# A two-layer decoder on one core: first projections start on their own weights, constant tables reordered and partly made by GpSimd, ScalarE's function table loaded early

## The reference

```
x = _layernorm(x + _L0_attn_ref(x, ...))        # 16 heads of 8, causal
x = _layernorm(x + _L0_xattn_ref(x, ctx, ...))  # 8 heads of 16, 64 context rows of width 96
x = _layernorm(x + _L0_ffn_ref(x, ...))         # router, 64 experts of width 88, 6 per token, and a shared one
x = _layernorm(x + _L1_attn_ref(x, ...))        # 16 heads of 64, causal
x = _layernorm(x + _L1_xattn_ref(x, ctx, ...))  # 16 heads of 64
x = _layernorm(x + _L1_ffn_ref(x, ...))         # an attention with nested widths, 8 heads of 16
```

```
qkv = x @ Wqkv.T
q, k, v = jnp.split(qkv, 3, axis=-1)          # then heads of 8
dots = einsum('bhid,bhjd->bhij', q, k) * scale
dots = jnp.where(causal_mask, -jnp.inf, dots)
attn = jax.nn.softmax(dots, axis=-1)
out = einsum('bhij,bhjd->bhid', attn, v)
return out @ Wout.T + bout
```

## Time and profile before

| | |
|---|---|
| time, three runs | 1831.59, 1843.01 (median), 1845.01 us |
| profiled execution | 1842.62 us, its span 1840.8 us |
| TensorE busy | 88% of the span |
| VectorE, ScalarE, GpSimd busy | 61%, 45%, 13% |
| granted TensorE clock, mean | 0.957 |
| first matmul, first scores | 20.54 us, 27.09 us |
| p1 until / experts until / p3 until | about 545, 654, 1841 us |

### The profile page before, as it was taken

One profiled execution on the slowest core, in us unless ns is written; L12 is line 12 of the kernel. 1 busy time (PEld: TensorE's weight loads), 2 busy tenths in 40 slices (PEclk: granted clock), 3 DMA queues, 4 the chain that ended last, 5 costly groups with the idle time before them and its releaser, 6 DMA issues.

```text
span 1840.8 us, 41666 instructions
## 1 busy us (share of the span) xinstructions
PE 1619.6 (88%) x17584; PEld 1056.4 (57%) x17616; DVE 1113.8 (61%) x2248; ACT 823.2 (45%) x1515; POOL 233.0 (13%) x392
## 2 busy tenths in 40 slices
PE   3799989999868968999998998998998998998985
PEld 1555555555537735665665665674674665665653
DVE  6187767777663454574575475485386387277353
ACT  1555655656522224444344345345445345435422
POOL 0011101111007600110010011011011011011011
PEclk9999999999978989999999999999999999999997
DMA  8421111111139440010010010011011011000000
GB/s 275 148 103 53 63 49 51 64 56 49 46 116 122 105 143 1 29 54 12 19 64 13 19 56 20 19 41 36 19 41 36 6 54 35 2 24 27 5 1 6
DMA packets 64809, 95.70 MB, mean 52 GB/s; under 512 B 9239, under 2 KB 47105, under 8 KB 63891
## 3 DMA queue, kind: packets, MB, share of 16 engines
q1 hardware_dynamic: 61491, 89.20, 14.6%
q0 software_dynamic: 2560, 3.46, 2.2%
q10 hardware_dynamic: 576, 0.39, 0.1%
HBM read 56.02 MB, written 38.80 MB: 52 GB/s over the span
## 4 chain that ended last, share of the span: by engine, by line
PE 57%; DVE 24%; ACT 7%; issue 6%; POOL 4%; DMA 1%; DVEq 0%; ACTq 0%; SPq 0%; POOLq 0%; PEldq 0%
PE psum L990 7%; PE psum L804 5%; DVE peak L1281 5%; PE psum L898 5%; ACT prob L1158 3%; PE psum L647 3%; PE psum L662 3%; PE psum L672 3%; PE psum L885 3%; PE psum L856 3%; DVE w_shared L1281 3%; PE psum L813 2%; PE psum L799 2%; POOL rstd L1456 2%; DVE kx L1406 2%
## 5 line engine op out<-in xcount | busy, mean ns | idle before, releaser
L1158 ACT ACTIVATE prob<-psum 128x1024 f32<-128x1024 f32 (+1 forms) x352 | 322.6, 945 | 354.2 <-PE psum L793 107.6
L1281 DVE TENSOR_REDUCE w_shared<-psum 128x4 bf16<-128x1024 f32 (+1 forms) x160 | 194.2, 1223 | 189.5 <-PE psum L711 125.0
L1281 DVE TENSOR_REDUCE peak<-psum 128x4 bf16<-128x1024 f32 (+1 forms) x160 | 190.8, 1218 | 18.0 <-PE psum L736 12.7
L1453 POOL TENSOR_TENSOR rstd<-moments,eps 128x2 f32<-128x2 f32 x64 | 15.3, 239 | 1018.6 <-DVE moments L1203 1018.6
L804 PE MATMUL psum<-qt,kt 64*128 64x256 f32 x1024 | 131.4, 376 | 0.0
L898 PE MATMUL psum<-prob,v_big 128*64 128x256 f32 x1024 | 124.6, 385 | 0.2 <-issue 0.2
L804 PEld LDWEIGHTS psum<-qt,kt 64*128 64x128 f32 x1024 | 98.5, 189 | 10.8
L898 PEld LDWEIGHTS psum<-prob,v_big 128*64 128x64 f32 x1024 | 68.0, 136 | 42.9 <-issue 11.9
L1309 DVE TENSOR_TENSOR qt<-qt,psum 128x1024 f32<-128x1024 f32 x32 | 38.3, 1218 | 84.7 <-PE psum L966 84.7
L939 PE MATMUL psum<-prob,va 128*32 128x256 f32 (+1 forms) x1536 | 88.9, 358 | 0.4 <-ACT prob L1158 0.2
L1102 ACT ACTIVATE kt<-psum,b_qk 128x256 f32<-128x256 f32 x128 | 53.6, 470 | 51.4 <-PE psum L662 51.0
(11 more groups left out here) (327 smaller groups left out, 3235.9 us busy)
## 6 DMA issues: line engine op xcount, KB each, us to landing
zd<-kx SPq DMA_DIRECT2D x24, 512.0 KB, 5.6
union<-zd SPq DMA_DIRECT2D x16, 768.0 KB, 4.5
w_late<-ad SPq DMA_DIRECT2D x16, 512.0 KB, 3.6
w_late<-vd SPq DMA_DIRECT2D x16, 512.0 KB, 4.6
ad<-union SPq DMA_DIRECT2D x16, 256.0 KB, 2.2
vd<-union SPq DMA_DIRECT2D x16, 256.0 KB, 2.3
xg<-union SPq DMA_DIRECT2D x16, 192.0 KB, 2.0
w_late<-in_w1T SPq DMA_DIRECT2D x1, 2816.0 KB, 11.1
```

The costliest lines, as they stand in the source:

```text
L1158: nc.scalar.activation(prob_of[a][s][:, slot + 2 * i:slot + 2 * i + 2, 0:n], v.pair(step, i)[:, :, 0:n], ACT.Exp, scale=a.scale).then_inc( ...
L1281: nc.vector.tensor_reduce(dst, src, axis=AX.X, op=ALU.max).then_inc(v.free(step), 1)
```

## The change

SyncE's queue begins with `w0_qkv` and both slots' `x`; the constants, the contexts and the other first weights follow, then `ctx_f`. TensorE waits for `w0_qkv` alone (`first_in`), and for the rest (`weights1_in`) ahead of its second step. ScalarE's queue loads four small strips of `ident` (`own_head`) ahead of the strips of `tri`, and ScalarE then runs one exponential on a column of `w0_qkv`, which brings the table load ahead of the first `qt`. GpSimd clears `wf_o`, `bf_o`, the zeros, `shift` and `rdiag`, and makes `sel_h`, `ident_b`, `upper_b` and `spread_b`; the first `T` step waits for them (`tables_ready`). VectorE makes only what the `S` steps and the masks need, and makes `ident_add`, `ones_x` and `shift` behind the experts' stage.

```diff
@@ tensor_step, kind "T"
+                if v.tag == "p1" and g == 0 and v.first():
+                    pe.wait_ge(tables_ready, 1)
...
@@ vector_step, kind "RN"
+                if v.first():
+                    dve.wait_ge(weights1_in, 16 * len(loads1))
...
-        loads1 = [(w0_qkv[:, :], "L0_Wqkv"), (b0_o[:, :], "L0_bout"), (wx_o, "L0_Wo")]
+        loads1 = [(b0_o[:, :], "L0_bout"), (wx_o, "L0_Wo")]
...
-        moved = [(tri_x[rows32(n), x, :], inp["tri"][rows32(n ^ x)]) for x in range(1, 4) for n in range(4)]
+        moved = [(own_head[r:r + 32, :], inp["ident"][r:r + 32, r:r + 16]) for r in range(0, 128, 32)]
+        moved += [(tri_x[rows32(n), x, :], inp["tri"][rows32(n ^ x)]) for x in range(1, 4) for n in range(4)]
...
@@ block.sync
+            sp.dma_start(w0_qkv[:, :], dram("L0_Wqkv")).then_inc(first_in, 16)
+            for s in AB:
+                load1(sp, s, s)
             for dst, name in consts:
                 sp.dma_start(dst, dram(name)).then_inc(consts_in, 16)
             for s in AB:
-                load1(sp, s, s)
                 load_context(sp, p1, s, s)
+            for dst, name in loads1:
+                sp.dma_start(dst, dram(name)).then_inc(weights1_in, 16)
             load_fold_context(sp, 0)
             sp.wait_ge(cleared, 1)
-            for dst, name in loads1:
-                sp.dma_start(dst, dram(name)).then_inc(weights1_in, 16)
...
@@ run_phase
+                            if tag == "p1" and it == -1 and (step[0], step[1]) != ("Q", L0) and not begun:
+                                eng.wait_ge(weights1_in, 16 * len(loads1))
+                                begun.append(step)
...
@@ block.tensor
-            pe.wait_ge(consts_ready, 1)
-            pe.wait_ge(weights1_in, 16 * len(loads1))
+            pe.wait_ge(first_in, 16)
...
@@ block.scalar
-            act.wait_ge(consts_ready, 1)
+            act.wait_ge(first_in, 16)
+            nc.scalar.activation(warm[:, :], w0_qkv[:, 0:1], ACT.Exp)
+            act.wait_ge(columns_set, 2)
...
@@ block.vector, ahead of p1
-            ms(wf_o[:, :, :], 0.0)
             for s in AB:
-                ms(shift[s][:, :, :], 0.0)
-                ms(rdiag[s][:, :, :], 0.0)
-                ms(xt_nested[s][:, :], 0.0)
...
             dve.wait_ge(consts_in, 16 * (len(consts) + len(moved)))
...
-            last.then_inc(consts_ready, 1)
-            dve.wait_ge(weights1_in, 16 * len(loads1))
+            ts(ident_inf[:, :], ident[:, :], 1.0e28, None, ALU.mult)
+            ts(tri_s[:, 0, :], tri[:, 0:128], -250.0, None, ALU.mult)
+            ts(tri_s[:, 1:3, :], tri_x[:, 1:3, 0:128], -250.0, None, ALU.mult)
+            ts(neg_ident[:, :], ident[:, :], -1.0, None, ALU.mult)
+            ts(tri_t[:, 0, :], tri[:, 128:256], -250.0, None, ALU.mult)
+            ts(tri_t[:, 1:4, :], tri_x[:, 1:4, 128:256], -250.0, None, ALU.mult).then_inc(masks_made, 1)
+            dve.wait_ge(masks_made, 1)
             run_phase(dve, "p1", vector_step)
             experts_vector(dve)
+            ts(ident_add[:, :], ident[:, :], 320.0, None, ALU.mult)
+            for u in AB:
+                cp(ones_x[rows64(u), :, :], ones_g[rows64(u), u, :, :])
+            for s in AB:
+                for r in (0, 64):
+                    for j in range(2):
+                        ts(shift[s][r:r + 32, j, 0:128], ident[r:r + 32, r + 31:r + 32].to_broadcast([32, 128]), -250.0, None,
+                           ALU.mult)
...
@@ block.gpsimd, ahead of p1
+            nc.gpsimd.memset(wf_o[:, :, :], 0.0)
+            nc.gpsimd.memset(bf_o[:, :, :], 0.0).then_inc(cleared, 1)
+            nc.gpsimd.memset(zeros, 0.0).then_inc(cleared, 1)
+            for s in AB:
+                nc.gpsimd.memset(shift[s][:, :, :], 0.0)
+                nc.gpsimd.memset(rdiag[s][:, :, :], 0.0)
+            copy = nc.gpsimd.tensor_copy
+            pool.wait_ge(consts_in, 16 * (len(consts) + len(moved)))
+            copy(sel_h[:, :, :], own_head[:, :].unsqueeze(2).to_broadcast([128, 16, 128]))
+            copy(ident_b[:, :], ident[:, :])
+            copy(upper_b[:, :], upper[:, :])
+            copy(spread_b[:, :, :], stage).then_inc(tables_ready, 1)
             pool.wait_ge(weights1_in, 16 * len(loads1))
```

More of the change, by code:

```diff
@@ L388, in decoder_program @@
         scale_v = sb("scale_v", [128, 4])
+        warm = sb("warm", [128, 1])
+        own_head = sb("own_head", [128, 16])
         by_layer = lambda own, cross: {a: cross if a is L0X else own for a in (L0, L0X, L1, L1X, L1F)}
@@ L433, in decoder_program @@
         weights_in = sem("weights_in")
-        consts_ready = sem("consts_ready")
+        tables_ready = sem("tables_ready")
         zeroed = sem("zeroed")
@@ L1954, in run_phase @@
         def run_phase(eng, tag, do_step, prepare=None):
+            begun = []
             def body(it, aheads):
@@ L2003, in _ @@
             ms, cp, ts = nc.vector.memset, nc.vector.tensor_copy, nc.vector.tensor_scalar
-            ms(wf_o[:, :, :], 0.0)
             for s in AB:
-                ms(shift[s][:, :, :], 0.0)
-                ms(rdiag[s][:, :, :], 0.0)
-                ms(xt_nested[s][:, :], 0.0)
-                ms(peak[s][:, :, :], 0.0)
-                ms(peak_x[s], 0.0)
-                ms(r_sel[s], BIG)
                 ms(va0[s], 0.0)
                 ms(va_x[s], 0.0)
-            ms(bf_o[:, :, :], 0.0).then_inc(cleared, 1)
-            ms(zeros, 0.0).then_inc(cleared, 1)
-            dve.wait_ge(cleared, 1)
+                ms(peak[s][:, :, :], 0.0)
+                last = ms(peak_x[s], 0.0)
+            last.then_inc(columns_set, 1)
+            for s in AB:
+                ms(r_sel[s], BIG)
+            dve.wait_ge(columns_set, 1)
             for s in AB:
@@ L2020, in _ @@
                 for i in range(2):
-                    ms(va_x[s][64 * i:64 * i + 64, :, 32 * i + 16:32 * i + 17], 1.0)
+                    last = ms(va_x[s][64 * i:64 * i + 64, :, 32 * i + 16:32 * i + 17], 1.0)
+            last.then_inc(columns_set, 1)
             dve.wait_ge(consts_in, 16 * (len(consts) + len(moved)))
-            ts(tri_s[:, 0, :], tri[:, 0:128], -250.0, None, ALU.mult)
-            ts(tri_t[:, 0, :], tri[:, 128:256], -250.0, None, ALU.mult)
-            ts(tri_s[:, 1:3, :], tri_x[:, 1:3, 0:128], -250.0, None, ALU.mult)
-            ts(tri_t[:, 1:4, :], tri_x[:, 1:4, 128:256], -250.0, None, ALU.mult)
-            cp(ident_b[:, :], ident[:, :])
-            cp(upper_b[:, :], upper[:, :])
-            cp(spread_b[:, :, :], stage)
-            ts(neg_ident[:, :], ident[:, :], -1.0, None, ALU.mult)
-            ts(ident_inf[:, :], ident[:, :], 1.0e28, None, ALU.mult)
-            ts(ident_add[:, :], ident[:, :], 320.0, None, ALU.mult)
-            for u in AB:
-                cp(ones_x[rows64(u), :, :], ones_g[rows64(u), u, :, :])
             nc.vector.tensor_reduce(slot_mask[:, 0:4], head_mask[:, 0:16].rearrange("p (j i) -> p i j", i=4), axis=AX.X,
@@ L2038, in _ @@
                                     op=ALU.add)
-            for r in range(0, 128, 32):
-                rows = slice(r, r + 32)
-                if r % 64 == 0:
-                    for s in AB:
-                        for j in range(2):
-                            ts(shift[s][rows, j, 0:128], ident[rows, r + 31:r + 32].to_broadcast([32, 128]), -250.0, None,
-                               ALU.mult)
-                last = cp(sel_h[rows, :, :], ident[rows, r:r + 16].unsqueeze(2).to_broadcast([32, 16, 128]))
-            last.then_inc(consts_ready, 1)
-            dve.wait_ge(weights1_in, 16 * len(loads1))
+            ts(ident_inf[:, :], ident[:, :], 1.0e28, None, ALU.mult)
[5 more added lines that the diff above has]
+            dve.wait_ge(masks_made, 1)
             run_phase(dve, "p1", vector_step)
             experts_vector(dve)
+            ts(ident_add[:, :], ident[:, :], 320.0, None, ALU.mult)
[6 more added lines that the diff above has]
+                           ALU.mult)
             for s in AB:
```

3 lines of the change are left out of this document (added).

## The result

The changed kernel takes 1829.64 us (median of 22 runs, 1825.86 to 1837.15), the kernel before on the same chips 1837.07 us (22 runs, 1828.17 to 1845.01). The ratio is 0.9958 with a 95% interval of 0.9946 to 0.997: some 7 us faster, clear of no change and under one per cent. Of the three runs of before that stand in the table two were among its slower ones, and the third (1831.59 us) among its faster; between the medians of 22 the difference is 7.4 us.

What follows compares the result with a forecast made beforehand. Bound: the head's chain, with VectorE's tables ahead of `kt`. Constants 12.4 us, tables to 13.8, GpSimd's hold 3.5, `kt` to scores 2.40: scores 19.7 instead of 27.09 us; 1842.62 - 7.4 = 1835.2 us (chance 0.45), range 1827 to 1843 us.

Steps and rivals of the forecast that it cites:

- the constants: Head: ScalarE's last strip load starts at 7.7 us and takes 4.73 us, so all constants are in at 12.4 us.
- GpSimd's copies: Head: GpSimd's four table copies, 3264 columns, take 4.5 us at half the rate of `x_res` for one input.
- VectorE's loss: Head: beside GpSimd's copies VectorE loses 0.79 us for each us, 3.5 us, so `kt` starts at 17.3 us.
- `kt` to scores: Head: from the start of `kt` to the first scores 2.40 us as before, so the scores come at 19.7 us.
- rival (f): Whole kernel: the change works but runs scatter over it, 13.4 us among three; chance of median over 1% faster 0.06, slower 0.03.
- ScalarE's table load: Head: its 1.28 us are done at 9.4 us, hidden behind the wait for the constants, and cost nothing.
- (a): Head: VectorE isn't held up by GpSimd's copies; 10.8 us gained, 1831.8 us; chance 0.15.
- (b): Head: GpSimd copies at the full rate of `x_res`; 7.0 us lost, 3.9 us gained, 1838.7 us; chance 0.15.
- (e): Head: GpSimd's copies hold VectorE past the old `kt` start, from 4.2 ns per column; 1845.8 us at 5.5 ns; chance 0.05.
- (c): Head: the first weights become the bound, in at 21.6 us; 5.5 us gained, 1837.1 us; chance 0.07.
- (d): Scores: TensorE's clock rise stays at about 57 us, some 2.5 us more at the lower level, 1837.7 us; chance 0.10.
- The experts' end: End of experts' stage: VectorE's 1.8 us of moved tables hide in its 6.33 us wait for routed rows, costing nothing.

Runs made afterwards that it cites:

- the loads alone: Changed kernel, but VectorE makes all tables ahead of `kt` in the order of before and GpSimd none: scores at 25.91 us, ratio 1.0013 to the kernel before.
- the first two experiments: Changed kernel with GpSimd's table copies held until VectorE's masks are made: scores 16.42 us; changed kernel with two more `sel_h`-shaped copies on GpSimd: `kt` at 20.13 us.
- the strips first: Changed kernel with ScalarE's queue loading the `own_head` strips behind those of `tri`, on a semaphore only GpSimd waits for: scores at 17.29 us, single run 1828.44 us.
- GpSimd behind VectorE: Changed kernel with GpSimd's four table copies waiting until VectorE has made its masks: scores at 16.42 us, ratio 0.9947 to the kernel before.
- The three versions with the strips first: Changed kernel with `tri` strips first: scores 17.29 us; plus GpSimd's copies behind masks and a later weights wait: 15.79; plus VectorE waiting only for its own constants: 15.15.

## Why the prediction was right

**The bound.** VectorE's tables were it, as read from the earlier trace rows (twelve kinds of table and not ten; no number of the sum hangs on that). The run with the loads alone shows it: projections at 6 us, scores at 25.9 us.

**The sum.** Forecast: scores at 19.7 us, 7.4 us gained. Measured: 19.79 us, 7.30 us in the head; 7.4 us between the medians. Term by term: the constants at 12.4 us, measured 13.14 (12.38 to 13.77 us in the eight profiles with the same loads ahead of them); GpSimd's copies 4.5 us, measured 3.52 us busy (1.89 + 0.29 + 0.24 + 1.10); VectorE's loss 3.5 us, measured 17.23 - 13.14 - 1.38 = 2.7 us, 0.77 for each microsecond against the 0.79 taken from the earlier trace rows; `kt` to scores 2.40 us, measured 2.56, the 0.15 us of the wait for the weights that the change put there. The errors, 0.7 and 0.2 us too little and 0.8 us too much, cancel, and that the scores came within 0.1 us of the forecast is luck; the step that carried the sum, that GpSimd's tables would hold VectorE's, was right and is shown by the first two experiments. The mis-sized term is the rate of GpSimd's one-input copies: 1.89 us for 2048 columns is 0.92 ns per column, where I took half of the two-input rate, 1.37, and looked for a copy of 2.9 us. The Trainium skill ("GPSIMD Engine Reference", "Engine selection") calls such work roughly line-rate; with the 1.2 GHz of its "Specifications" that is an estimate of 0.83 ns per column. The trace agrees within the fixed part of an instruction: from 1024 columns (1.04 us with VectorE idle, 16.23 to 17.27 us in the run with the strips first) to 2048 (1.89 us) a column costs 0.83 ns.

**The absolute time** was off by 5.6 us (1835.2 against 1829.64 us), although inside the range: the profiled execution that I subtracted from lay 5.6 us above the median of 22 runs. That is rival (f), and the reason that the range had to be wider than the terms.

**ScalarE's table load.** I costed it as hidden by the wait for the constants. It is hidden, but the edit isn't what hides it: without it the load is at the same place, behind the DMA issues.

**The rivals.** (a), VectorE not held: refuted by the rows. (b) and (e), slower copies: 0.92 ns per column, against 2.73 and 4.2. (c), the weights: in at 16.23 and 16.6 us in the two chains that show it, as forecast, hidden by over 3 us in the changed kernel and level with VectorE's chain as soon as GpSimd's copies were out of the way. (d), the clock: these rows of the changed kernel answer to the earlier trace rows:

```profile
25.00:30.00 5.00, 2.22 (x30) 0.47 (x30) 4.05 (x4) 1.52 (x3) 0.00 (x0) 0.95 0.17 38
30.00:35.00 5.00, 4.29 (x36) 1.97 (x36) 2.81 (x3) 0.95 (x3) 0.00 (x0) 0.50 1.02 406
...
50.00:55.00 5.00, 3.12 (x88) 2.09 (x80) 0.00 (x0) 2.59 (x5) 0.00 (x0) 1.00 1.03 409
55.00:60.00 5.00, 4.17 (x72) 2.51 (x76) 0.00 (x0) 2.23 (x4) 0.00 (x0) 0.69 1.01 398
```

```profile
45.92 1.52 PE L860 MATMUL psum<-qt,kt 32*128 32x256 f32 x16
...
49.96 0.85 PE L860 MATMUL psum<-qt,kt 32*128 32x256 f32 x16
...
60.13 0.89 PE L860 MATMUL psum<-qt,kt 32*128 32x256 f32 x16
```

The granted clock (PEclk) is 0.50 in the windows from 30 to 50 us and 1.00 in the next, and the group of L860 falls from 1.52 to 0.85 us at 49.96 us, 7.06 us before the same group of the earlier trace rows. In the other profiles, with scores between 15.15 and 25.91 us, the first group that takes 0.82 or 0.83 us starts 29.9 to 33.7 us behind the scores (in the kernel before, 29.9). So the rise from 1.2 to 2.4 GHz came with the work, not at a fixed time, and (d) as forecast cost nothing. The Trainium skill ("TensorE: Matmul & The Clock Gate", "What's actually happening") says that activity releases the clock, and the trace agrees. But this profile has one more stretch at the lower level (0.69 in the window of 55 to 60 us): the group at 55.99 us is 7.0 us ahead of its fellow in the kernel before, the next, at 60.13 us, only 5.9 us. The second profile of the changed kernel doesn't have it (the same group at 59.08 us, 6.95 us ahead). So the clock took back over 1 us of the gain in one execution and nothing in another; it is one of the sources of the scatter.

**The experts' end.** Nothing lost, as costed; the cover is there, 5.94 and 4.67 us deep in the two profiles, where I had 4.5 us.

## What to carry to other kernels

A wait that stands ahead of a stage is worth splitting only as far as the next bound: here the early projections and loads brought 1.2 us alone (25.91 us against 27.09), because VectorE's tables were the bound, and some 2 us once those were short (22.09 against 19.79 us). The short tables were the larger part, 5.0 us alone and 6.1 us with the early projections. Each step's next bound could be read beforehand from when the loads land, to within 0.9 us. When tables are handed to GpSimd so that VectorE gets done sooner, they should not start on the same semaphore: held back until VectorE's last mask they cost it nothing (`kt` took its usual 1.23 us), and nobody waits for them for another 20 us (`sel_h` made at 16.84 us, used at 35.63 us). A gain of 0.4% is seen in the rows of the head at once, in the medians only with 6 to 22 runs of a kernel beside 14 to 22 of the other.

## What the runs showed of the hardware that I had not expected

GpSimd and VectorE can hold each other for whole instructions, in both directions: `ident_inf` 1.83 us beside `sel_h` in place of 0.22, `sel_h` 2.87 us beside `kt` in place of 1.89, `kt` 2.54 us beside `sel_h` in place of 1.23. Reduces on small tiles (0.18 and 0.15 us) and `peak` reduces out of PSUM (1.23 us at 17.66 us beside `spread_b` and `x_res`, GpSimd behind VectorE) kept their times. So did one table: `tri_t` from the strips ran 0.54 us, its usual time, from 16.66 us in the changed kernel beside GpSimd's first `x_res` addition (16.58 to 17.32 us). Alone it is slower per column than the tables that were held (0.47 us to the next start for 384 columns, against 0.20 us for 256 of `tri_s`); whether that is the reason isn't tested. The Trainium skill ("SBUF — State Buffer", "SBUF: two separate sides") says that of GpSimd and a VectorE operation that uses the shared ports whoever starts first has them for its whole instruction, and the rows agree in each place where one was held. With casts queued on GpSimd and tables on VectorE they took turns, one for one, which left VectorE one operation per cast, for casts of 0.3 us and of 1.9 us. And TensorE's clock, in the changed kernel's trace, went up once before: three matmul groups at 26 to 28 us ran at the higher level (L744 in 0.39 us, 0.61 at 30.71 us), and the window of 25 to 30 us reads 0.95, that behind it 0.50. The three versions with the strips first show the same short rise 6 to 8 us behind their scores (L744 in 0.39 us at 24.73, 23.23 and 22.59 us), the other eight profiles don't.
